# A decoder layer on one core: x kept on chip, queries stored in three parts, denominators spread by a product, a middle stage three chunks deep, weights transposed by the host

## The chip, the core and the metric

The kernel runs on one core of one Trainium2 chip. A core has a matrix engine (TensorE, PE in the profile, its weight loads as PEld), a vector engine (DVE), an activation engine (ACT), a general engine (POOL) and a sync engine (SP) that issues most DMA transfers here. Each engine runs its own instructions in the order written, and they meet through semaphores. The metric is the device time of one execution in microseconds (us), lower is better. Before the change it is 1234.29 us, the median of three runs (1232.31 to 1235.03).

## The reference

One pre-norm decoder layer over 4 sequences of 1024 tokens, 256 features, 16 heads of 16. Where the given mask is true, the score is set to -1e9.

```python
def self_attn(x):                       # x normalised
    Q, K, V = x @ Wq.T + bq, x @ Wk.T + bk, x @ Wv.T + bv        # (b, s, 16, 16)
    scores = (gt * einsum(Q, W_cross, K) + (1 - gt) * einsum(Q, M @ K)) * 16 ** -0.5
    # M: 16 x 16 a head, shift_weights at offsets 0 to 7; gt = sigmoid(gate)
    scores = where(causal, scores, -inf)
    return (softmax(scores) @ V) @ Wo.T + bo
def cross_attn(x, ctx, masked):         # ctx: 77 tokens a sequence
    q, k, v = x @ Wq, ctx @ Wk, ctx @ Wv
    return (softmax(where(masked, -1e9, q @ k.T / 4)) @ v) @ Wo
def ffn(x):                             # hidden 768, int32 weights / 127
    return (silu(x @ wg.T) * (x @ wu.T)) @ wd.T
x = x + self_attn(norm(x)); x = x + cross_attn(norm(x), ctx, mask); x = x + ffn(norm(x))
```

## The kernel before

The 4096 tokens are worked on as 8 chunks of 512, and attention as 16 groups of 4 heads (4 groups for each sequence). The program is a row of blocks. At the end of each all engines meet, so nothing of a block starts before every engine has left the one ahead; the function `barrier` adds such a meeting at the same places.

1. **Weights** (0 to about 50 us). All inputs are loaded. The projection weights are transposed on TensorE (L489) and emptied by ACT (L444) and DVE (L382). `W_cross`, the shift weights and the gate are folded into the query weights (DVE L387 to L415). Keys and values of the context are made. The FFN's integer weights are converted (ACT L450), transposed, and split in a high and a low part. ACT and PE begin when all loads up to the cross-attention weights have landed.
2. **Q/K/V chunks** (50 to 134.7 us). For each chunk x is loaded, normalised (DVE L215), transposed (L1208), and multiplied by the weights (L178). Queries and keys are split in three bf16 parts that add up to the f32 value; values get a column of ones (L1128 writes them, `a_vst`, 32 columns a head of which 17 hold data). All goes to DRAM (`qk`, `vs`).
3. **Self-attention** (134.7 to 668.2 us). For each group, a ring of 40 units of *maxima* (L753 for scores, L762 for the causal part, then the DVE maximum L677), whose row `self_mrow` travels by DMA (L627) into two extra rows of the queries `self_stq`. Then 38 *score* units (L776, L784), for which ACT takes the exponential (L728), and 12 sets of *value products* (L796): the exponentials stream against f32 value tiles `self_va` of 32 columns, four heads side by side. ACT empties a set (L720), SP stores it (L649, `od`, numerators and denominators). SP loads the groups' inputs with L958, L962 and L869: 19 transfers a group.
4. **Middle** (668.2 to 801.2 us). For each chunk the quotients `oin` x `din` are made (L909; `din` is the inverse denominators, which a DMA L845 has read from DRAM once for each of the 16 columns of a head). Then the projection (L986), the residual sum (L1415, with x loaded again as `rin`), moments (L157 to L168), a power on POOL (L1369), the normalisation (DVE L1429), transposes (L1500), transposes of the mask (L1506), and the query product (L1516), split in three bf16 parts (L1483, L1436, L1439, L1374). The parts are stored in six slots by 48 transfers from the queues of SP and ACT (L1299), and the new x is stored too (L1326). Two chunks are under way at a time. DVE also works out which tokens are fully masked (L1401 to L1406), with padding of a sequence to 96 context columns.
5. **Cross-attention** (801.2 to about 964 us). The same ring as in stage 3, without the causal part, on 96 context columns a head, L758 adding the mask.
6. **FFN** (to 1233.9 us). The denominators, the projection and the normalisation of `c`, then the three large products (L178) for each chunk.

What sets the order around the change: each engine's own list, written by hand as loops (`chunk c`, `unit u`), and the meetings between blocks. The class `ChunkInputs` (L873) holds the loads of `oin`, `din` and `rin`, the quotients and the projection for both stage 4 and stage 6; its `early_...` methods run a first chunk's part inside the attention block's last group. SP's list in the last group of stage 3 or 5 thus holds the loads of the next stage's first two chunks (L843, L845, L903), at the last two of four points:

```python
                if i == 2:
                    sp.wait_ge(self.s_inv, 32)
                    self.load(sp, 0, 0)
                if i == 3:
                    self.load(sp, 0, 1)
```

## Time and profile before

| | before |
|---|---|
| median of three runs | 1234.29 us |
| profiled execution | 1235.59 us |
| span of its trace | 1233.9 us |
| mean granted TensorE clock | 0.947 of full speed |
| PE busy, PEld busy | 1076.2 us (87%), 633.6 us (51%) |
| DVE, ACT, POOL busy | 788.9, 556.0, 215.9 us |

The span runs from the first to the last instruction in the trace, and the profiled execution's own time is 1.7 us longer. In the rows below, *windows* give the busy time of each engine in a stretch with its number of instructions, then the granted TensorE clock as a share of full speed, the busy share of the DMA engines, and GB/s. A *timeline* row is: start, duration, engine, line, operation, out<-in, count (neighbouring instructions of one kind are one row), and in brackets the idle time ahead with what ended it. A row of *lines by form* is one kind of instruction in a stretch: busy us in all and mean ns of one, then the engine's idle us ahead of it and what released it. *Waits* give us in all, times and the longest. A matrix product in f32 appears as two passes, so x16 in a timeline is 8 products in the program.

### The profile page before, as it was taken

How to read it: one execution, taken by the hardware profiler on the slowest of the kernel's cores; microseconds unless marked ns; L12 is line 12 of the kernel's file. 1: busy time of each engine (PE TensorE's matmuls, PEld its weight loads, DVE VectorE, ACT ScalarE, POOL GpSimd, SP SyncE). 2: the span in 40 equal slices, each digit the busy share in tenths (PEclk: the TensorE clock that was granted, in tenths of full speed). 3: DMA queues.
4: the chain of work that ended last, by engine and by line, in shares of the span. 5: the costliest groups of instructions: out<-in, count | busy, mean ns of one | idle time of the engine just before them, and what ended most of it. 6: DMA issues, size and time to landing. Idle time of an engine off the chain costs nothing. (4 is left out here: it accounts for less than half of the span.)

```text
span 1233.9 us, 19626 instructions
## 1 busy us (share of the span) xinstructions
PE 1076.2 (87%) x7164; PEld 633.6 (51%) x7164; DVE 788.9 (64%) x1705; ACT 556.0 (45%) x1022; POOL 215.9 (17%) x175
## 2 busy tenths in 40 slices
PE   1889969999999999999997656669999599999997
PEld 1677424444444444444433434334444278888886
DVE  4699847777777777777872757655556254554452
ACT  2455126666666666666674111216666321111110
POOL 4155510000000000000001334310000133333321
PEclk9899769999999999999999887779999789999999
DMA  6389993434443344443022786865664422222200
GB/s 198 98 286 306 271 150 75 82 86 84 87 89 86 86 86 85 82 88 80 23 75 86 207 240 187 244 217 179 177 182 131 158 61 69 69 70 69 69 18 35
DMA packets 132831, 153.28 MB, mean 124 GB/s; under 512 B 29003, under 2 KB 104319, under 8 KB 132735
## 3 DMA queue, kind: packets, MB, share of 16 engines
q1 hardware_dynamic: 126207, 145.74, 45.5%
q10 hardware_dynamic: 6528, 6.29, 1.5%
q8 instruction: 57, 0.93, 0.3%
q14 instruction: 39, 0.32, 0.1%
HBM read 87.69 MB, written 64.95 MB: 124 GB/s over the span
## 5 line engine op out<-in xcount | busy, mean ns | idle before, releaser
L677 DVE TENSOR_REDUCE self_pm<-bank 128x1 f32<-128x512 f32 (+3 forms) x608 | 365.0, 657 | 95.4 <-PE bank L762 74.5
L728 ACT ACTIVATE self_prob<-bank 128x512 f32<-128x512 f32 (+1 forms) x608 | 325.6, 577 | 170.7 <-PE bank L784 97.0
L776 PE MATMUL bank<-self_stq,self_stk 98*128 98x512 bf16 (+3 forms) x768 | 223.1, 331 | 16.0 <-DMA self_stq<-self_mrow 10.7
L753 PE MATMUL bank<-self_stk,self_stq 96*128 96x512 bf16 (+3 forms) x768 | 227.4, 339 | 9.1 <-DVE self_mrow L674 6.6
L796 PE MATMUL bank<-self_prob,self_va 128*32 128x512 f32 (+3 forms) x1536 | 161.4, 500 | 0.0
L753 PEld LDWEIGHTS bank<-self_stk,self_stq 96*128 96x128 bf16 x768 | 70.6, 99 | 160.9 <-DVE self_pm L677 114.2
L951 POOL TENSOR_TENSOR rin<-rin,bo_b 128x1024 f32<-128x1024 f32 x8 | 26.1, 3260 | 528.0 <-DMA min_<-mask_BxSxS_bk 528.0
L1758 ACT ACTIVATE e_sg<-bank 128x512 f32<-128x512 f32 x48 | 28.8, 599 | 192.1 <-PE bank L178 192.1
L776 PEld LDWEIGHTS bank<-self_stq,self_stk 98*128 98x128 bf16 x768 | 69.6, 99 | 75.4 <-issue 20.7
L728 ACT ACTIVATE cross_prob<-bank 96x512 f32<-96x512 f32 x128 | 74.5, 591 | 60.6 <-PE bank L781 60.4
L677 DVE TENSOR_REDUCE cross_pm<-bank 128x4 f32<-128x384 f32 x128 | 69.5, 557 | 33.3 <-PE bank L758 31.8
L762 PE MATMUL bank<-tri_q,identb 128*128 128x128 bf16 (+2 forms) x352 | 88.1, 250 | 0.0
L784 PE MATMUL bank<-tri_k,identb 128*128 128x128 bf16 (+2 forms) x352 | 86.4, 245 | 0.0
L986 PE MATMUL bank<-wo_t,oin 128*128 128x256 f32 x128 | 42.2, 501 | 45.9 <-DVE oin L909 40.6
L178 PE MATMUL bank<-e_xnt,wg_t 128*128 128x512 f32 x288 | 78.5, 408 | 1.4 <-DVE e_xnt L1711 1.4
L1674 POOL TENSOR_TENSOR e_ht<-e_hf,e_ht 128x512 fp32r<-128x512 f32 x48 | 62.6, 1303 | 76.7 <-DVE e_ht L1705 76.7
L178 PE MATMUL bank<-e_xnt,wu_t 128*128 128x512 f32 x288 | 75.8, 398 | 0.0
L178 PE MATMUL bank<-wd_t,e_ht 128*128 128x256 f32 x576 | 70.5, 282 | 3.2 <-POOL e_ht L1674 3.2
L178 PEld LDWEIGHTS bank<-wd_t,e_ht 128*128 128x128 f32 x576 | 70.1, 188 | 4.3 <-POOL e_ht L1674 3.7
L1703 DVE TENSOR_TENSOR e_hf<-bank,e_sg 128x512 f32<-128x512 f32 x48 | 33.1, 690 | 54.2 <-ACT e_sg L1758 42.3
L986 PEld LDWEIGHTS bank<-wo_t,oin 128*128 128x128 f32 x128 | 32.6, 262 | 57.6 <-DVE oin L909 45.6
L178 PEld LDWEIGHTS bank<-e_xnt,wu_t 128*128 128x128 f32 x288 | 54.8, 190 | 13.5
(189 smaller groups left out, 1418.0 us busy)
## 6 DMA issues: line engine op xcount, KB each, us to landing
qk<-a_parts SPq DMA_DIRECT2D x32, 384.0 KB, 4.9
self_stq<-qk SPq DMA_DIRECT2D x192, 64.0 KB, 3.0
self_stk<-qk SPq DMA_DIRECT2D x96, 128.0 KB, 5.2
cross_stq<-xqs SPq DMA_DIRECT2D x32, 384.0 KB, 4.7
vs<-a_vst SPq DMA_DIRECT2D x8, 1024.0 KB, 7.2
self_va<-vs SPq DMA_DIRECT2D x16, 512.0 KB, 7.3
od<-self_u SPq DMA_DIRECT2D x16, 512.0 KB, 2.6
oin<-od SPq DMA_DIRECT2D x32, 256.0 KB
```

Of the source, the lines that this page charges most:

```text
L178: mm = nc.tensor.matmul(dst, a[:, i], b[:, j], start=(n == 0), stop=(n == 3 * len(terms) - 1))
L677: nc.vector.tensor_reduce(pm[:, k, h0:h0 + hb, r], src[:, 0:hb * w].rearrange("p (h w) -> p h w", h=hb), AX, ALU.max).then_inc(s_mxe, 1)
L728: nc.scalar.activation(ops.prob[:, u % NPS, 0:hb * n], bank[ST_BANKS[u % 3]][0:KP, 0:hb * n], ACT.Exp).then_inc(s_ex, 1)
L753: mm = nc.tensor.matmul(dst[:, h * w:(h + 1) * w], stq[i][0:R, half, h0 + h, r * P:(r + 1) * P], stk[i][0:R, h0 + h, k0:k0 + w], start=(h ...
L762: mm = nc.tensor.matmul(dst[:, 0:hb * w].rearrange("p (h w) -> p h w", h=hb)[:, :, w - P:w], identb[:], tri_q[:, 0:hb], start=False, stop= ...
L776: mm = nc.tensor.matmul(dst[0:KP, h * n:(h + 1) * n], stk[i][0:RM, h0 + h, kt * KP:(kt + 1) * KP], stq[i][0:RM, half, h0 + h, q0:q0 + n], ...
L784: mm = nc.tensor.matmul(dst[:, 0:hb * n].rearrange("p (h n) -> p h n", h=hb)[:, :, 0:P], identb[:], tri_k[:, 0:hb], start=False, stop=True ...
L796: mm = nc.tensor.matmul(bank[PV_BANKS[half]][h * VW:(h + 1) * VW, q0:512], va[i][:, kt, h * VW:(h + 1) * VW], ops.prob[:, (first + h // hb ...
L986: mm = nc.tensor.matmul(bank[w][:, i * D:(i + 1) * D], oin[:, u, k, (2 * w + i) * P:(2 * w + i + 1) * P], wo_t[:, k], start=(k == 0), stop ...
L1674: nc.gpsimd.tensor_tensor(ht[:, u, 1, h], hf[:, h % 2], ht[:, u, 0, h].bitcast(F32), ALU.subtract).then_inc(s_hl, 1)
L1703: nc.vector.tensor_tensor(hf[:, h % 2], bank[5 + 2 * (h % 2)][:], sg[:, h % 2], ALU.mult).then_inc(s_h, 1)
L1758: nc.scalar.activation(sg[:, h % 2], bank[4 + 2 * (h % 2)][:], ACT.Silu).then_inc(s_sg, 1)
```

## The change

- **Weights.** The host hands over `Wk`, `Wv`, `Wo`, the FFN weights, the context and the mask already transposed, so the transposes of block 1 go. SP and ACT both issue the loads, in another order, and the gate is among the first. The conversion of the FFN weights moves into the middle stage (ACT makes the high part, POOL the low part).
- **x kept on chip.** x is loaded once into `xres` (8 chunks), POOL adds the bias, the residual sums are made in place. The loads `rin` and the stores `x1s` go.
- **Values.** `a_vst` and `va` hold 17 columns a head instead of 32, with the four heads innermost: the columns of one head's weight tile lie 16 bytes apart in memory instead of side by side.
- **Self-attention.** A group's inputs come by 10 transfers instead of 19. Groups 0 and 1 are loaded during the q/k/v chunks, 2 and 3 from ACT's queue. The banks of the ring carry on over a group's end, and the last value products of a group are issued among the first units of the next.
- **Denominators.** A bf16 product of the inverses `rd` with a 0/1 matrix `sel` (L922) writes the spread inverses into a bank, and DVE multiplies from there (`quotients`).
- **Middle.** The projection runs three chunks ahead of the query product. Normalisation is on ACT, POOL makes power and offset, the mask comes as one tile, the queries go out in three parts by 2 transfers a chunk. In the last self-attention group six spreads and two projections run ahead (before: one projection).
- **Cross-attention** works on 80 context columns, keys and mask of all groups are resident, and the FFN's first inputs are loaded after group 6 of the 16.

```diff
@@ layout and DRAM tensors
-    SK = 96
+    SK = 80
+    VC = HD + 1
-    x1s = dram("x1s", (NCH, P, J, D), F32)
-    xqs = dram("xqs", (B, KT, len(Q_PARTS), HD, HP, S), BF16)
+    rd3 = dram("rd3", (B, 3, H, S), BF16)
+    xq3 = dram("xq3", (B, KT, 3, P, S), BF16)
+        xres = sb(root, "xres", [P, NCH, J, D])
@@ weights: the transposes on TensorE go, the host does them
-            turned(n_k, both(wk_t), KT, KT)
-            turned(n_v, both(wv_t), KT, KT)
-            turned(n_o, (wo_t,), KT, KT)
-            turned(fg, both(wg_t), KT, HT)
-            turned(fu, both(wu_t), KT, HT)
-            turned(fd, both(wd_t), HT, KT)
+        ("Wk_t", rows_first(given["L0_attn_Wk"].T)),
+        ("Wv_t", given["L0_attn_Wv"].T),
+        ("Wo_t", given["L0_attn_Wo"].T),
+        ("gate_t", given["L0_ffn_w_gate"].T),
+        ("up_t", given["L0_ffn_w_up"].T),
+        ("down_t", given["L0_ffn_w_down"].T),
@@ values: 17 columns a head, heads innermost
-            vst = sb("a_vst", [P, 2, GB, J, HG, VW])
+        vst = sb(qkv, "a_vst", [P, 2, GB, J, VC, HG])
@@ loads of a self-attention group
-            for slot, part in enumerate(Q_PARTS):
-                for c in range(2):
-                    sp.dma_start(stq[HD * slot:HD * (slot + 1), c],
-                                 qk3[0, part, bass.ds(g, 1), :, c * 512:(c + 1) * 512]
-                                 .rearrange("a (h r) t -> (a r) h t", h=HG)).then_inc(ld, 16)
+            for slot, first, number in Q_RUNS:
+                for c in range(2):
+                    eng.dma_start(stq[i][HD * slot:HD * (slot + number), c],
+                                  qk3[0, b, i // 2, first:first + number, :, c * 512:(c + 1) * 512]
+                                  .rearrange("c (r h) s -> (c r) h s", h=HP)[:, heads]).then_inc(ld[i], 16)
@@ SP at the start of self-attention
-                barrier(sp, 2)
-                load_group(sp, self_ops, 0, 1)
-                self_sync(sp, True)
-                load_group(sp, self_ops, 0, 2)
-                self_sync(sp, False)
+                qkv_sync(sp)
+                barrier(sp, 1)
+                self_sync(sp)
+            for i in range(2, GB):
+                a.wait_ge(s_set, i + 1)
+                load_self(a, i)
@@ order of the products, and the bank of a unit
+            plan += [("p", s, -1) for s, x in enumerate(sets) if x[3] - 1 == NST + u - LAG]
-                    dst = bank[MX_BANKS[n % 3]]
+                dst = bank[MXB[N % NMB]]
+        early(8, lambda t: spread(t, 0, 0))
+        early(10, lambda t: spread(t, 0, 1))
+        early(13, lambda t: project2(t, 0))
+        early(15, lambda t: spread(t, 1, 0))
+        early(18, lambda t: spread(t, 1, 1))
+        early(22, lambda t: project2(t, 1))
+        early(26, lambda t: spread(t, 2, 0))
+        early(30, lambda t: spread(t, 2, 1))
@@ denominators by a product
-                eng.tensor_tensor(oin[:, u], oin[:, u], din[:, u], ALU.mult).then_inc(self.s_on, 1)
+        def spread(t, c, k):
+            b, u = c // 2, c % 2
+            t.wait_ge(s_rl, 16 * (b + 1))
+            n = KT * c + k
+            need(t, s_on, n if c < N_EARLY else n - 1)
+            nc.tensor.matmul(bank[EB if c < N_EARLY else BB[k]][:], sel[:, k], rd[:, b, u * CH:(u + 1) * CH],
+                             start=True, stop=True).then_inc(s_bc, 1)
+        def quotients(v, c, k):
+            v.wait_ge(ldo[c % 3], 32 * (c // 3 + 1))
+            v.wait_ge(s_bc, KT * c + k + 1)
+            nc.vector.tensor_tensor(oin[:, c % 3, k], bank[EB if c < N_EARLY else BB[k]][:], oin[:, c % 3, k],
+                                    ALU.mult).then_inc(s_on, 1)
@@ middle stage
-                for slot, number in Q_RUNS:
-                    eng.dma_start(xqs[bass.ds(b, 1), n, slot:slot + number, :, :, u * CH:(u + 1) * CH]
-                                  .rearrange("a s r h t -> (a r h) s t"),
-                                  parts[:, u, n, 0:number]).then_inc(so[n][u], 16)
+                sp.dma_start(xq3[b, n, :, :, u * CH:(u + 1) * CH].rearrange("c p s -> p c s"),
+                             cparts[:, u, n]).then_inc(cso[u], 16)
+            t.wait_ge(s_u, 2 * G)
+            t.wait_ge(s_on, KT * N_EARLY)
+            for k in range(KT):
+                spread(t, 3, k)
+            project2(t, 2)
+            turn(0)
+            for c in range(NCH):
+                t.wait_ge(cs_xt, KT * (c + 1))
+                for n in range(KT):
+                    need(t, cs_r, KT * (c - 1) + n + 1)
+                    for k in range(KT):
+                        mm = nc.tensor.matmul(bank[QB[n]][:], xwq[:, k, n * P:(n + 1) * P], cxnt[:, c % 2, k],
+                                              start=(k == 0), stop=(k == KT - 1))
+                    mm.then_inc(cs_q, 1)
+                if c + 4 < NCH:
+                    for k in range(KT):
+                        spread(t, c + 4, k)
+                if c + 1 < NCH:
+                    turn(c + 1)
+                if c + 3 < NCH:
+                    project2(t, c + 3)
+            t.wait_ge(cs_xt, KT * NCH)
+            t.wait_ge(cs_r, KT * NCH)
+                    for k in range(KT):
+                        quotients(v, c + 4, k)
+                if c + 3 < NCH:
+                    sums2(v, c + 3)
+        def mid_scalar(a):
+            def normalise(c):
+                a.wait_ge(cs_nm, c + 1)
+                need(a, cs_tr, KT * (c - 1))
+                for j in range(J):
+                    nc.scalar.activation(cxn[:, c % 2, j], xres[:, c, j], ACT.Identity,
+                                         scale=crstd[:, c % 3, j:j + 1],
+                                         bias=cneg[:, c % 3, j:j + 1]).then_inc(cs_xn, 1)
@@ inputs of the last stage
-                if i == 2:
-                    sp.wait_ge(self.s_inv, 32)
-                    self.load(sp, 0, 0)
-                if i == 3:
-                    self.load(sp, 0, 1)
+                    store_inverse(sp, b)
+                    if b == 0:
+                        load_ffn(sp, 0)
+                        load_ffn(sp, 1)
```

TensorE's list in the middle stage, two chunks of the kernel before (`oin` are the quotients, `c_xn` the normalised chunk, `c_xnt` its transpose, `c_meff` the mask):

```order
L986 MATMUL bank<-wo_t,oin 128x256 x8
L1500 MATMUL bank<-ident,c_xn 128x128 x8
L1506 MATMUL bank<-identb,c_meff 96x128 x4
L1516 MATMUL bank<-c_xnt,xwq 128x512 x4
L986 MATMUL bank<-wo_t,oin 128x256 x8
L1500 MATMUL bank<-ident,c_xn 128x128 x8
L1506 MATMUL bank<-identb,c_meff 96x128 x4
L1516 MATMUL bank<-c_xnt,xwq 128x512 x4
```

The same engine and stage after the change, from its first row on (`rd` are the inverse denominators, `sel` the 0/1 matrix):

```order
L922 MATMUL bank<-rd,sel 128x512 x2
L937 MATMUL bank<-wo,oin 128x256 x8
L1097 MATMUL bank<-ident,c_xn 128x128 x8
L1112 MATMUL bank<-c_xnt,xwq 128x512 x4
L922 MATMUL bank<-rd,sel 128x512 x2
L1097 MATMUL bank<-ident,c_xn 128x128 x8
L937 MATMUL bank<-wo,oin 128x256 x8
L1112 MATMUL bank<-c_xnt,xwq 128x512 x4
```

Before, a chunk's projection, transposes and query product follow one another. After, the row L937 is for the chunk three ahead of the query product L1112 behind it, and the transposes are for the next one.

SP's list where self-attention begins, before (from the last store of the q/k/v chunks to the loads of group 1):

```order
L1079 DMA vs<-a_vst 128x4x512
L958 DMA self_stq<-qk 16x4x512 x12
L962 DMA self_stk<-qk 16x4x1024 x6
L869 DMA self_va<-vs 128x1024
L627 DMA self_stq<-self_mrow 1x16x128 x2
L958 DMA self_stq<-qk 16x4x512 x12
L962 DMA self_stk<-qk 16x4x1024 x6
L869 DMA self_va<-vs 128x1024
L627 DMA self_stq<-self_mrow 1x16x128 x2
```

and after:

```order
L248 DMA qk<-a_parts 128x3x512 x4
L251 DMA vs<-a_vst 128x4x272
L676 DMA stq<-mrow 1x16x128 x8
L681 DMA od<-u_out 128x1024
L663 DMA stq<-qk 48x4x512 x2
L663 DMA stq<-qk 32x4x512 x2
L663 DMA stq<-qk 16x4x512 x2
L667 DMA stk<-qk 48x4096
```

The maxima's transfers (L627, now L676) no longer have 19 loads of a group ahead of them on SP: the first loads stand earlier in the list, inside the q/k/v stores, and two groups' loads are on ACT's list.

TensorE's list in the last self-attention group, after (`prob` are the exponentials, `va` the values, `tri_k` the causal part):

```order
L814 MATMUL bank<-stq,stk 128x384
L818 MATMUL bank<-tri_k,identb 128x128
L922 MATMUL bank<-rd,sel 128x512
L814 MATMUL bank<-stq,stk 128x256 x2
L818 MATMUL bank<-tri_k,identb 128x2x128
L814 MATMUL bank<-stq,stk 128x256 x2
L818 MATMUL bank<-tri_k,identb 128x2x128
L922 MATMUL bank<-rd,sel 128x512
L814 MATMUL bank<-stq,stk 128x128 x4
```

The spreads L922 stand between score units, as do two projections further on.

## Rows read from the trace of the kernel before

**Rows 1.** Windows: us; busy us of PE, PEld, DVE, ACT, POOL; clock; DMA; GB/s.
```profile
134.70:165.00 30.30, 20.64 (x71) 5.66 (x72) 22.93 (x45) 0.00 (x0) 13.96 (x5) 0.59 0.91 241
165.00:668.20 503.20, 488.47 (x3753) 209.25 (x3753) 365.54 (x680) 338.70 (x639) 5.76 (x2) 0.98 0.40 82
668.20:818.90 150.70, 88.19 (x355) 57.04 (x356) 98.89 (x261) 22.55 (x41) 48.48 (x34) 0.82 0.73 221
818.90:964.00 145.10, 134.72 (x1079) 66.59 (x1079) 77.55 (x199) 86.95 (x154) 0.00 (x0) 0.97 0.58 163
964.00:986.50 22.50, 9.57 (x39) 5.65 (x39) 6.97 (x17) 3.50 (x7) 5.66 (x3) 0.71 0.45 155
986.50:1233.90 247.40, 238.51 (x1328) 207.51 (x1328) 118.64 (x249) 38.14 (x65) 83.79 (x61) 0.98 0.20 57
```

**Rows 2.** Timeline, DVE and PE at the start: start, us, engine, line, names.
```profile
14.25 0.24 DVE L387 TENSOR_SCALAR ge<-ge 128x2 f32<-128x2 f32 x1 [14.25 <-ACT ge L440]
...
22.75 0.29 DVE L415 TENSOR_TENSOR ablk<-ablk,blk 128x128 f32<-128x128 f32 x1
...
46.95 1.06 PE L1208 MATMUL bank<-ident,a_xn 128*128 128x128 f32 x8 [3.05 <-SPq L1031]
50.22 5.28 PE L178 MATMUL bank<-a_xnt,wq_t 128*128 128x512 f32 x12 [2.20 <-DVE a_xnt L1101]
```

**Rows 3.** Timeline of DVE and PE in a chunk of the q/k/v stage.
```profile
62.23 1.41 DVE L1128 TENSOR_TENSOR a_vst<-bank,bv_b 128x256 f32<-128x256 f32 x4
...
65.86 1.09 PE L1208 MATMUL bank<-ident,a_xn 128*128 128x128 f32 x8 [1.02 <-DVE a_xn L215]
```

**Rows 4.** Timeline of SP's queue ahead of self-attention.
```profile
158.03 5.73 SPq L958 DMA_DIRECT2D self_stq<-qk  x12
```

**Rows 5.** Waits of PE, 134 to 668: total us, times, longest.
```profile
PE bank L776 <- DMA self_stq<-self_mrow: 10.7, 2, 7.9
PE bank L753 <- DVE self_mrow L674: 6.6, 15, 1.0
PE bank L776 <- ACT self_prob L728: 4.9, 18, 0.3
```

**Rows 6.** Lines by form, 300 to 580: busy us, mean ns | idle us.
```profile
L796 PE MATMUL bank<-self_prob,self_va 128*32 128x512 f32 x432 | 57.5, 605 | 0.0
...
L796 PEld LDWEIGHTS bank<-self_prob,self_va 128*32 128x32 f32 x864 | 17.9, 108 | 31.3 <-ACT self_prob L728 16.8 <-issue 12.9
```

**Rows 7.** Timeline of PE in the middle stage.
```profile
705.37 3.72 PE L986 MATMUL bank<-wo_t,oin 128*128 128x256 f32 x16 [1.82 <-DVE oin L909]
709.90 1.09 PE L1500 MATMUL bank<-ident,c_xn 128*128 128x128 f32 x8 [0.81 <-DVE c_xn L1429]
...
711.79 3.70 PE L1516 MATMUL bank<-c_xnt,xwq 128*128 128x512 f32 x8 [0.57 <-ACT c_xnt L1473]
...
742.79 6.29 PE L986 MATMUL bank<-wo_t,oin 128*128 128x256 f32 x16 [8.37 <-DVE oin L909]
```

**Rows 8.** Lines by form, 667 to 802 us.
```profile
L986 PE MATMUL bank<-wo_t,oin 128*128 128x256 f32 x112 | 38.5, 518 | 45.9 <-DVE oin L909 40.6 <-DVE c_x L1415 5.3
...
L157 DVE BATCH_NORM_STATS2 c_stat<-c_x 128x6 f32<-128x256 f32 x32 | 11.2, 414 | 0.3
...
L1415 DVE TENSOR_TENSOR c_x<-bank,rin 128x512 f32<-128x512 f32 x16 | 10.2, 678 | 0.3 <-issue 0.3
...
L1473 ACT ACTIVATE c_xnt<-bank 128x512 f32<-128x512 f32 x16 | 8.7, 594 | 86.9 <-PE bank L1500 86.9
...
L1369 POOL TENSOR_TENSOR c_rstd<-c_ve,mhalf 128x4 f32<-128x4 f32 x8 | 8.1, 1017 | 35.6 <-DVE c_ve L168 35.6
```

**Rows 9.** Lines by form, 819 to 964 us.
```profile
L753 PE MATMUL bank<-cross_stk,cross_stq 96*128 96x96 bf16 x448 | 37.7, 207 | 7.3 <-DVE cross_mrow L674 5.1 <-DMA cross_mk<-mts 2.2
L758 PE MATMUL bank<-negid,cross_mk 96*128 96x384 bf16 x112 | 37.1, 331 | 0.0
```

**Rows 10.** Timeline of POOL behind cross-attention.
```profile
969.52 2.34 POOL L909 TENSOR_TENSOR oin<-oin,din 128x1024 f32<-128x1024 f32 x1 [163.66 <-DMA rin<-x1s]
```

More of the change, by code:

```diff
@@ L529, in attention @@
-        def attention(stage, name, causal, ahead, ops, o_dst, following):
-            KW = S if causal else SK
-            KP = P if causal else SK
-            NKT = S // P if causal else 1
-            NPS = 12
-            mx_units = []
+        s_xh = sem("a_xh")
+        s_xt = sem("a_xt")
+        s_qk = sem("a_qk")
+        s_hi = sem("a_hi")
+        s_r = sem("a_r")
+        s_m = sem("a_m")
+        s_lo = sem("a_lo")
+        s_vm = sem("a_vm")
+        s_ve = sem("a_ve_")
+        so = sems("a_so", 2)
@@ L559, in attention @@
                     st_units += [(half, kt, h, hb, q0, n, diag) for h in range(0, HG, hb)]
-                    sets.append((half, kt, first, len(st_units), kt == kts[0], kt == kts[-1], q0, n, hb))
-            NST = len(st_units)
-            half_end = [max(s[3] for s in sets if s[0] == h) for h in range(2)]
-            ring = [("m", i) for i in range(len(mx_units))]
-            ring.insert(min(n_half + (4 if causal else 2), len(ring)), ("t", 0))
-            ring.append(("t", 1))
-            NMX = len(ring)
@@ new lines, in cross_scalar, with outputs @@
+        def cross_scalar(a):
+            def outputs(g, c):
+                if c == 0:
+                    need(a, xus[g % 2], 16 * (g // 2))
+                a.wait_ge(xs_pv, g * NST2 + HG * (c + 1))
+                nc.scalar.activation(xu[:, g % 2, c * 512:(c + 1) * 512], bank[PVB[c]][:],
+                                     ACT.Identity).then_inc(xs_u, 1)
+            for g in range(G):
+                for u in range(NST2):
+                    U = g * NST2 + u
+                    a.wait_ge(xs_st, U + 1)
+                    need(a, xs_pv, U + 1 - NPS2)
+                    nc.scalar.activation(xprob[:, U % NPS2], bank[STB[U % NSB]][0:SK, :], ACT.Exp).then_inc(xs_ex, 1)
+                    if u == NST2 - 1:
+                        outputs(g, 0)
+                    if g and u == LAG2:
+                        outputs(g - 1, 1)
+            outputs(G - 1, 1)
@@ L1361, in _ @@
+        cross_left.close()
+        cross.close()
+        last = root.enter_context(ExitStack())
+        yo = sb(last, "e_yo", [P, 2, J, D])
+        exnt = sb(last, "e_xnt", [P, 2, 2, KT, CH], F32R)
+        sg = sb(last, "e_sg", [P, 2, CH])
+        hf = sb(last, "e_hf", [P, 2, CH])
+        ht = sb(last, "e_ht", [P, 2, 2, HT, CH], F32R)
+        with nc.Block() as block:
+            @block.sync
+            def _(sp):
+                ffn_sync(sp)
                 barrier(sp, 4)
```

2768 lines of the change are left out of this document (1373 added, 1395 removed).

## The prediction

> **What bounds the kernel now.** I read the span in windows first [rows 1]. In self-attention, cross-attention and the FFN PE is busy nearly all the time: 488.5 of 503.2 us, 134.7 of 145.1 and 238.5 of 247.4, at a clock of 0.97 or 0.98. An edit there pays only if it takes work off PE. The rest is where PE waits: the head, up to 50.22 us, when the first q product runs [rows 2]; the entry to self-attention, 134.7 to 165, 20.6 busy of 30.3 at a clock of 0.59; the middle stage with the meeting behind it, 668.2 to 818.9, 88.2 busy of 150.7; and the passage to the FFN, 9.6 of 22.5. Second, the waits of PE and the rows by line say what ends the idle time, and third the timelines give one pass of each loop. In all of them the reader is to see the idle time in brackets and the name behind it: in the middle stage nearly all of it is the quotients `oin` (45.9 us, 40.6 of them L909) [rows 8], which are late because their inputs come through DRAM.
>
> **The head.** DVE starts folding at 14.25, held by ACT's gate row L440, and ends the fold at 22.75 + 0.29, 8.8 us for some 20 dependent rows [rows 2]. ACT waited for all loads up to the cross-attention weights. Afterwards the gate is the third kind of load and nothing else is waited for; I take 7 for DVE's start, half of 14.25, since half of the loads stand ahead of it. The two folds are interleaved, so I take 8.3 instead of 8.8: done at 15.5. What stood between the fold and the first transposes at 46.95 was nearly all weight transposes and the integer weights, which go. What stays are the statistics, the power on POOL, the normalisation and the context products. Statistics are four of 0.41 us [rows 8] and six small rows of about 0.2 (an estimate from the 0.24 of L387), the power 1.0 [rows 8], normalisation about as long as the statistics: 1.7 + 1.2 + 1.0 + 1.7 = 5.6, so transposes at 21. From the transposes to the first q product it took 50.22 - 46.95 = 3.3 [rows 2]; with context products of about 2 between, the first q product stands at 26. That is 24 us earlier. Bounds: 18 (start at 10, the context products in the way with their copies) and 28.
>
> **The q/k/v chunks.** x is there already, the products are the same. One idle gap of 1.02 us a chunk [rows 3] could go (8 x 1.02 = 8 gained); against that the writes of the values, 1.41 us a chunk [rows 3], are now at a pitch of four elements and could take twice as long, 8 x 1.4 = 11 lost if nothing covers them. I take 0, nearest to the products that do not change, and keep +11 and -8.
>
> **Entry to self-attention.** PE waited twice, 10.7 us in all, for rows of the maxima that travel by SP [rows 5]; SP had 12 transfers of L958 in front, 5.73 us [rows 4], and six of L962 behind. After the change SP has only the maxima's transfers at its head. I count -10.7; up to 8 more could come if PE's 20.6 busy us in rows 1 at a clock of 0.59 run at 0.98 (20.6 x (1 - 0.59/0.98)), and up to 2 could be lost on ACT, whose 20 transfers stand ahead of exponentials.
>
> **Group boundaries.** PE waited 15 times for `self_mrow`, 6.6 us, and 18 times for ACT's exponentials, 4.9 us [rows 5]: one each at the 15 borders between groups, and the others beside them. The ring carries on over the border now. Of the 11.5 I count 9.
>
> **Value products.** The weight tile has 17 columns instead of 32, 16 bytes apart. A load took 108 ns, its product 605 [rows 6], and the load is covered by the product ahead in most sets. I take 0: fewer columns, each of them costlier. Half of the 864 loads' 17.9 us in rows 6 is 9, for a window of 280 of 503 us, so 16 over the stage is the largest gain if none were covered; I take 13 to either side. The Trainium skill speaks against this edit: "Advanced Engine Details and Errata", section Memory Cachelines, has lines of 16 bytes in SBUF, of which two hits each are needed for full speed and where a new line for each access costs extra. By that rule every column of a load is on a line of its own, where before four shared one; by the row alone (108 ns, covered) nothing is lost. No trace of before has a strided load, so none can say how much. What such a penalty would need to turn the result is the slower rival below.
>
> **Last self-attention group.** One more projection (3.72 for a chunk, rows 7) and six spreads come in, 3.7 + 6 x 0.2 = 5. A spread is one bf16 product of 512 columns; from L753 with 96 columns, 207 ns, to L758 with 384, 331 ns [rows 9], a column costs 0.43 ns, so 0.22 us. Count +5; both ends 3 and 7.
>
> **The middle stage.** For a chunk PE has the projection 3.72, the transposes 1.09, the query product 3.70 [rows 7] and two spreads 0.44; the mask's transposes go. That is 8.9 us, if the projection runs three ahead and nothing is late. DVE has two quotients and two sums (each like L1415, 0.68), statistics 4 x 0.41, six small rows of 0.2, two splits of 0.68: 6.8 us, so DVE is close behind but covered. POOL's power and multiplication take 2 x 1.02 [rows 8] against 1.02 before, ACT's two copies of the transposes (L1473) 2 x 0.59. Walk: meeting 1.3 us, spreads and a projection 4.1, transposes 1.1 and copies: the first query product ends at about 11. The loads of the outputs of chunk 3 are issued only when the last group's stores have landed, 8 us in, and DVE takes the quotients of chunk 3 ahead of the sums of chunk 2, so the second is later than PE's pace: about 19. Four chunks at 8.9 follow: 19 + 4 x 8.9 = 54.6. The last two have no projections but their own copies and sums, 7.9 and 6.6, and a last product with its split and stores 3.7: 73. The two stages before have 150.7 with the meeting [rows 1]; of these the entry to cross-attention I take at 16, for stores and maxima's transfers still stand there: 73 + 16 = 89, so -61.7. Bounds: 83 (PE's 8 x 8.9 = 71, less the projection of the head, + 14) and 125 (below). The cover is thin: the queries' split and DVE's order have two chunks of slack at most, and if it is gone, a chunk costs what the chain from quotients to normalisation costs.
>
> **Cross-attention.** 80 columns instead of 96 a head: 16 x 4 fewer in the score rows (L753) and as many in L758, 128 columns a unit, x 0.43 ns [rows 9] = 55 ns; 128 units: 7.0. The wait for `cross_mrow`, 5.1 [rows 9], goes with the continued ring. Count -12; bounds -4 and -14.
>
> **Passage to the FFN.** PE is busy 9.6 of 22.5 us [rows 1]. POOL began the quotients at 969.52, when `rin` had landed, after 2.34 us of work each chunk [rows 10]. With x resident and the first inputs loaded since group 6, the quotients can be made in the attention stage's last groups. What stays is the meeting, the chain of projection, sums, power, normalisation, transposes: 3.7 + 1.4 + 2.9 + 2 + 1.7 = 11.5. Count -11; bounds -4 and -13. The FFN itself (247.4) has the same products: 0.
>
> **Sum.** -24 + 0 - 10.7 - 9 + 0 + 5 - 61.7 - 12 - 11 = -123.4. The profiled execution took 1235.59, so 1112.2; the median of the runs stands 1.3 lower (1234.29), so 1110.9, say 1111. The measurement of this kernel can tell a change from none above about 0.2%, 2.5 us.
>
> **The rivals.** *A, the forecast:* 1095 to 1128, as worked out. *B, the middle stage does not reach PE's pace.* DVE at 6.8 us of 8.9 takes its work strictly in order, the spread for chunk c+4 waits for a bank that DVE empties, and ACT and POOL get the FFN weights' conversion on top (1536 columns three times each). If a chunk takes about 12 us, 8 x 3.1 = 25 are lost; if the loads of outputs come behind the queries' stores too, up to 36 more: 1128 to 1165. For it: in rows 7 the projection waits 8.37 us for DVE behind a long chain, and then runs slower (6.29 for the same 16 rows that took 3.72) at a stage clock of 0.82. Against it: three chunks of slack, and half the stores. *C, better:* the gaps of rows 3 go (8), loads of values shrink (13), the entry's clock rises (8): 1070 to 1095. *D, slower than before:* strided value loads on PE's path. There are 16 x 12 = 192 sets of 8 loads (four heads, two passes). To lose all 123 us, a set must take 0.64 us longer, or 80 ns a load if nothing covers it: a load of about 190 ns instead of 108 [rows 6]. From there on the kernel is slower; at 250 ns it takes 1111 + 192 x 8 x 0.142 = 1329. Against it: a load with covered start and 17 columns instead of 32 would need to cost more than three times as much a column. *E, part of the change does nothing:* the head stays (the FFN weights or x hold it) or the middle is bound by transfers throughout, 1165 to 1231.
>
> **How the numbers follow.** A 0.52, B 0.25, C 0.15, E 0.03, D 0.04, and 0.01 for a time within 0.2% of before. The prediction is A's, 1111. Range: all of A, most of B and of C, 1080 to 1152, leaving out a third of B, the last quarter of C, D and E, together 0.08 + 0.04 + 0.07, just under 0.2. Faster: A + B + C + E = 0.95, of which I move 0.01 to slower for other unseen faults: 0.94, within 0.2% 0.01, slower 0.05.
>
> **What would show it.** In the profile after: the first q product at 24 to 30 us; PE without a wait for a maxima row over 2 us at the entry; in self-attention the value loads' mean near 100 ns (D: near 200 or more) and the stage's busy share above 97%; in the middle stage one query product each 9 us from the second on, no wait of PE above 2 us, a clock above 0.82 (B: 12 us a chunk, PE idle by quotients or sums); the passage to the FFN at 11 to 12 us. I am wrong if the head's gain is under 15 or the middle's under 40, and in direction only by way of the value loads.

## The result and the profile after

The kernel after takes 1252.86 us (median of three runs, 1251.66 to 1254.38) against 1234.29 before. The ratio is 1.0155 with a 95% interval of 1.0129 to 1.018: slower by 1.6%, where 1111 was forecast and 1080 to 1152 was the range. The span of the profiled execution is 1251.1 us, and the mean granted clock is 0.87 instead of 0.947.

The windows of the kernel after, cut where the same work begins and ends as in [rows 1] (length, then busy us of PE, PEld, DVE, ACT, POOL, then clock, DMA share, GB/s):

```profile
33.35:116.60 83.25, 75.37 (x442) 64.09 (x440) 72.78 (x173) 47.32 (x78) 42.69 (x38) 1.00 0.76 223
116.60:642.80 526.20, 511.99 (x3846) 217.82 (x3846) 410.14 (x772) 341.25 (x641) 30.45 (x17) 0.97 0.37 76
642.80:749.20 106.40, 74.74 (x317) 45.00 (x317) 48.88 (x136) 54.14 (x88) 43.59 (x33) 0.84 0.57 156
749.20:1002.80 253.60, 241.51 (x1117) 100.84 (x1117) 76.99 (x214) 90.35 (x159) 5.70 (x3) 0.51 0.36 80
1002.80:1007.60 4.80, 1.12 (x12) 0.86 (x8) 2.64 (x6) 2.54 (x4) 0.00 (x0) 0.83 0.28 112
1007.60:1251.10 243.50, 236.06 (x1320) 208.69 (x1320) 116.74 (x246) 36.02 (x63) 83.61 (x61) 0.98 0.14 44
```

| stage | before | after | change | forecast |
|---|---|---|---|---|
| head, to the first q product | 50.2 | 33.35 | -16.9 | -24 |
| q/k/v chunks | 84.5 | 83.25 | -1.2 | 0 |
| self-attention | 533.5 | 526.2 | -7.3 | -14.7 |
| middle and entry to cross-attention | 150.7 | 106.4 | -44.3 | -61.7 |
| cross-attention | 145.1 | 253.6 | **+108.5** | -12 |
| passage to the FFN | 22.5 | 4.8 | -17.7 | -11 |
| FFN | 247.4 | 243.5 | -3.9 | 0 |

Every stage but one is shorter. Cross-attention alone takes 108.5 us more, at a granted clock of 0.51 of full speed where it was 0.97 [rows 1], although PE is busy 241.5 of 253.6 us. The same products by form, in cross-attention after:

```profile
L1339 PE MATMUL bank<-xstq,xstk 98*80 98x512 bf16 x119 | 75.7, 636 | 0.0
L1341 PE MATMUL bank<-mk,negid 80*80 80x512 bf16 x118 | 74.8, 634 | 0.0
```

The same two in cross-attention before:

```profile
L776 PE MATMUL bank<-cross_stq,cross_stk 98*96 98x512 bf16 x125 | 49.8, 398 | 4.3 <-PEq L1255 4.3
L781 PE MATMUL bank<-cross_mk,negid 96*96 96x512 bf16 x125 | 48.3, 386 | 0.0
```

They took 398 and 386 ns and now take 636 and 634, with 80 columns of weights instead of 96. The clock fell at the end of the middle stage and stayed at 1.2 GHz (0.50 of full speed) until the first projection of the FFN:

```profile
730.00:735.00 5.00, 3.72 (x41) 2.26 (x41) 3.98 (x12) 0.20 (x1) 1.67 (x2) 0.79 0.46 159
735.00:740.00 5.00, 4.44 (x39) 3.14 (x40) 3.75 (x12) 0.00 (x0) 0.00 (x0) 0.50 0.01 3
740.00:745.00 5.00, 0.66 (x6) 0.27 (x4) 1.34 (x4) 0.00 (x0) 0.00 (x0) 0.50 0.42 81
745.00:750.00 5.00, 0.79 (x2) 0.21 (x2) 0.00 (x0) 0.00 (x0) 0.00 (x0) 0.50 0.56 82
750.00:995.00 245.00, 233.69 (x1080) 96.92 (x1080) 73.38 (x200) 88.04 (x155) 4.69 (x2) 0.50 0.37 80
```

The projection's products have 128 rows and 128 columns of weights, and from 996 on the clock is 1.00 again:

```profile
994.21 4.38 PE L1454 MATMUL bank<-xwo,oin 128*128 128x256 f32 x16
```

The idle stretch from 740 to 749 is a wait for the maxima, and four waits for queries stand behind it, the longest of 6.7 us. Waits of PE in the kernel after, from 725 to 1000 us (total, times, longest):

```profile
PE bank L1339 <- DMA xstq<-xmrow: 8.6, 1, 8.6
PE bank L1326 <- DMA xstq<-xq: 7.9, 4, 6.7
```

The kernel before falls to the low clock at the same place, at about 816 us, and leaves it again after about 10 us. Its windows:

```profile
820.00:825.00 5.00, 2.84 (x15) 1.71 (x16) 1.06 (x3) 1.19 (x2) 0.00 (x0) 0.50 0.55 144
825.00:830.00 5.00, 5.00 (x39) 2.62 (x37) 2.77 (x7) 2.96 (x5) 0.00 (x0) 0.85 0.51 124
830.00:835.00 5.00, 4.45 (x41) 2.16 (x37) 2.36 (x7) 2.44 (x5) 0.00 (x0) 1.00 0.17 66
```

So the question was not why the clock fell, but why it did not come back. The change did two things to this stage that could matter: 80 columns and rows a head instead of 96, and another order of loads and waits.

### The profile page after: what moved, and what is told of

The parts are those of the page before. It is cut to its first block and busy times, and to the rows that moved or that the text cites. A ratio compares the mean times of both kernels' runs of the same rounds, so it can differ in the third digit from the quotient of the medians.

```text
span 1251.1 us, 19036 instructions
## 1 busy us (share of the span) xinstructions
PE 1151.4 (92%) x7092; PEld 645.8 (52%) x7092; DVE 748.7 (60%) x1603; ACT 577.7 (46%) x1043; POOL 230.2 (18%) x191
## 5 line engine op out<-in xcount | busy, mean ns | idle before, releaser
L726 DVE TENSOR_REDUCE pm<-bank 128x1 f32<-128x512 f32 (+3 forms) x608 | 364.6, 656 | 83.6 <-PE bank L802 63.4
L774 ACT ACTIVATE prob<-bank 128x512 f32<-128x512 f32 (+1 forms) x608 | 329.2, 575 | 184.0 <-PE bank L818 105.2
L797 PE MATMUL bank<-stk,stq 96*128 96x512 bf16 (+3 forms) x768 | 227.2, 340 | 7.3 <-DVE pm L726 4.1
L814 PE MATMUL bank<-stq,stk 98*128 98x512 bf16 (+3 forms) x768 | 222.4, 328 | 0.9 <-ACT prob L774 0.8
L828 PE MATMUL bank<-prob,va 128*17 128x512 f32 (+3 forms) x1536 | 164.0, 500 | 0.0
L1305 ACT ACTIVATE xprob<-bank 80x512 f32<-80x512 f32 x128 | 75.7, 592 | 181.6 <-PE bank L1341 181.3
L1339 PE MATMUL bank<-xstq,xstk 98*80 98x512 bf16 x128 | 80.7, 631 | 8.6 <-DMA xstq<-xmrow 8.6
L1341 PE MATMUL bank<-mk,negid 80*80 80x512 bf16 x128 | 80.4, 628 | 0.0
L132 PE MATMUL bank<-e_xnt,wg 128*128 128x512 f32 x288 | 76.7, 402 | 1.6 <-DVE e_xnt L1507 1.6
L132 PE MATMUL bank<-e_xnt,wu 128*128 128x512 f32 x288 | 74.4, 394 | 0.0
```

What stands on the lines that cost most here:

```text
L132: mm = nc.tensor.matmul(dst, a[:, i], b[:, j], start=(n == 0), stop=(n == 3 * len(terms) - 1))
L726: nc.vector.tensor_reduce(pm[:, k, h0:h0 + hb, r], src[:, 0:hb * w].rearrange("p (h w) -> p h w", h=hb), AX, ALU.max).then_inc(s_mxe, 1)
L774: nc.scalar.activation(prob[:, U % NPS, 0:hb * n], bank[STB[U % NSB]][:, 0:hb * n], ACT.Exp).then_inc(s_ex, 1)
L797: mm = nc.tensor.matmul(dst[:, h * w:(h + 1) * w], stq[i][0:R, half, h0 + h, r * P:(r + 1) * P], stk[i][0:R, h0 + h, k0:k0 + w], start=(h ...
L814: mm = nc.tensor.matmul(dst[:, h * n:(h + 1) * n], stk[i][0:RM, h0 + h, kt * P:(kt + 1) * P], stq[i][0:RM, half, h0 + h, q0:q0 + n], start ...
L828: mm = nc.tensor.matmul(bank[PVB[half]][h * VW:h * VW + VC, q0:512], va[g % GB][:, kt, :, h], prob[:, (g * NST + first + h // hb) % NPS, ( ...
```

## The experiments

A ratio is the time against the kernel before, measured beside it, with its 95% interval behind it. The diffs are cut to the lines that matter.

### First round: 80 or 96, and the idle stretch

Theory T1: products on 80 rows or columns don't bring the clock back once it has fallen. Rival T2: the clock stays down because of the idle stretch and the thin work ahead of the stage, whatever the tile. `a_sk96` is the kernel after with 96, `a_sk88` with 88, and `b_sk80` is the kernel before with 80; each is one line:

```diff
-    SK = 80
+    SK = 96
```

`a_fill8` puts products on the full array into the idle stretch at the entry:

```diff
+            for n in range(8):
+                nc.tensor.matmul(bank[PVB[1]][:], ident[:], xwo[:].rearrange("p k d -> p (k d)"), start=True, stop=True)
             for g in range(G):
                 for what, which, ahead in plan2:
```

> The kernel before with 80 context columns and rows a head in cross-attention instead of 96: that part of the change alone. T1: the clock, which falls to 0.5 around 820 us in the kernel before, doesn't come back in cross-attention, and the kernel takes 1330 to 1350 us. T2: it comes back as in the kernel before, and the kernel takes 7 us less, about 1227.

Measured: 1324.7 us (ratio 1.074, 1.070 to 1.078), a little under T1's range and 91 us slower than the kernel before beside it (1233.3). Its windows in cross-attention, the last of which takes in the first projection of the FFN:

```profile
810.00:820.00 10.00, 4.78 (x33) 2.45 (x30) 4.21 (x13) 0.59 (x1) 0.00 (x0) 0.50 0.87 248
820.00:840.00 20.00, 18.50 (x91) 8.33 (x92) 6.05 (x16) 6.53 (x11) 0.00 (x0) 0.50 0.31 85
840.00:1080.00 240.00, 228.04 (x1044) 97.49 (x1042) 76.61 (x203) 90.16 (x151) 5.66 (x3) 0.52 0.36 102
```

This is T1: with one constant changed and the old order of loads and waits, the clock stays at 0.5 for the whole stage (0.50 from 805 to 1060). The constant sets the rows and the columns of several products at once; no run tells which of them counts.

> The kernel after with 96 context columns and rows a head in cross-attention instead of 80, all else as it is. Theory T1 (products on 80 rows or columns don't bring TensorE's clock back once it has fallen): the stage runs at a clock near 1 again, about 145 us instead of 252, and the kernel takes 1135 to 1150 us. Theory T2 (the clock stays down because of the idle 8.6 us and the thin work ahead of the stage, whatever the tile size): clock 0.5 as before, and some 7 us more, about 1260.

Measured: 1252.33 us (ratio 1.0166, 1.0118 to 1.0215), no gain, with executions from 1247.8 to 1259.3. Both theories failed as written: the clock was neither near 1 nor at 0.5. It rose and fell again and again. Waits and windows of this run:

```profile
PE bank L1326 <- DMA xstq<-xq: 20.5, 9, 4.5
```

```profile
760.00:770.00 10.00, 9.14 (x79) 4.53 (x82) 5.71 (x15) 5.81 (x11) 0.00 (x0) 1.00 0.08 28
770.00:780.00 10.00, 5.86 (x42) 2.84 (x38) 2.92 (x8) 2.64 (x6) 0.00 (x0) 0.72 0.59 108
780.00:800.00 20.00, 19.69 (x90) 8.15 (x91) 6.15 (x15) 6.30 (x11) 0.00 (x0) 0.50 0.33 67
800.00:820.00 20.00, 19.69 (x96) 9.16 (x94) 7.29 (x19) 7.94 (x14) 0.00 (x0) 0.53 0.39 90
```

In the fast stretch PE has 9.1 us of work in 10, and then the queries of the group after next come late: PE waits 3.3 us for `xstq<-xq`, up to 776.8, and the clock falls. While the clock is low most of these loads are in time (no such wait from 777 to 818, and in the kernel after four waits of 7.9 us in all against nine of 20.5 here), so it hides the fault. So there is a second cause, which 80 columns had covered. The last two windows show a thing more: at 96 too PE was busy 39.4 of 40 us at the low clock, and it took until 818 to come back. What 96 has over 80 is that the clock did come back, after every fall but the last, 31 us ahead of the projection; it did not do so at once.

Part of the lateness comes from another piece of the change. With the queries stored in three parts instead of six slots, SP issues six transfers for a group where it issued two. The load in this run, then in the kernel before:

```profile
768.96 3.29 SPq L1210 DMA_DIRECT2D xstq<-xq  x6
```

```profile
853.79 1.11 SPq L969 DMA_DIRECT2D cross_stq<-xqs  x2
```

That is 2.2 us more; what of the wait of 3.3 us it makes was not tested apart from the place of the load in SP's list.

> The kernel after with eight f32 products of 128 x 128 x 512 put in front of the first scores of cross-attention, into a bank that nothing uses yet, where PE idles 8.6 us. T1: the clock rises during them and is back at 0.5 soon after, with 80 columns: 1250 to 1262 us. T2: with the idle stretch filled the clock stays up, about 1140 to 1150 us.

Measured: 1247.1 us (1.0108, 1.0075 to 1.0141), 3 us under T1's range. The clock rose and was 1.00 from 760 to 770 with 80 columns, then fell at the same wait for queries (3.9 us; 0.73 from 770 to 780, PE busy 5.4 of 10 us) and stayed at 0.50 to the end of the stage. T2 is out, and 80 columns did run at the high clock until a gap came.

> The kernel after with 88 context columns and rows a head. T1: either as with 96 (about 1140) or as with 80 (about 1256); a value between, by a stage partly at the low clock, is possible at the edge. T2: about 1256.

Measured: 1257.27 us (two executions), clock 0.50 in every window from 740 to 1000. 88 behaves as 80 does.

### Second round: a fifth query buffer

`n5_sk96` and `n5_sk80` load a group's queries one group earlier (the fifth buffer itself and the indices are left out here):

```diff
-        xld = sems("d_ld", GB)
+        NX = 5
+        xld = sems("d_ld", NX)
-                        load_cross(sp, g + GB - 1)
+                        load_cross(sp, g + NX - 1)
```

> The kernel after with 96 context columns and five query buffers in cross-attention instead of four, so that a group's queries are loaded one group earlier. Theory T1b (two causes: the late query loads let the clock fall again and again, and products on 80 rows never bring it back): no wait for xstq<-xq over 1 us, the clock near 1 for the whole stage, some 145 us for it instead of 252, the kernel 1135 to 1155 us. Rival T3 (the clock falls by the mix of the work itself, two groups ahead, whatever the waits): still 0.5 to 0.75 in many stretches, 1230 to 1250 us.

Measured: 1185.72 us (0.9593, 0.9552 to 0.9633), 67 us less than `a_sk96`, but 30 more than the top of T1b's range; the executions spread from 1178.6 to 1200.6. No wait for `xstq<-xq` was left. The clock was 1.00 from 760 to 810 and fell at two gaps, of 2.9 and 6.8 us; it was back after about 4 us in the first case and 24 in the second:

```profile
816.57 0.95 DVE L1408 RECIPROCAL den<-den 128x128 f32<-128x128 f32 x1 [4.85 <-DMA den<-od]
817.44 0.15 DVE L1266 COPY xmrow<-bank 32x128 bf16<-32x128 bf16 x1
...
817.64 0.34 PE L1328 MATMUL bank<-xstk,xstq 96*128 96x96 bf16 x4 [2.92 <-DVE xmrow L1266]
...
846.56 0.66 PE L1341 MATMUL bank<-xstq,xstk 98*96 98x512 bf16 x1 [6.80 <-DMA xstq<-xmrow]
```

First, DVE's reciprocal of the denominators waits 4.85 us for its load, and the copy that the maxima need is queued behind it. Second, both of the FFN's first chunks are loaded in one go, and SP's transfers of the maxima are queued behind them.

> The kernel after with five query buffers alone, 80 columns kept. T1b: the clock falls at the entry of cross-attention, as before, and doesn't come back although nothing is waited for: 1240 to 1252 us, the gain only the waits of 8 us. Rival T2b (without the late loads the clock comes back at 80 columns too): 1130 to 1150 us.

Measured: 1246.93 us (1.0115, 1.0083 to 1.0146): T1b. No wait for queries was left, and the clock stayed at 0.50 from 750 to 985.

> Five query buffers, 80 columns, and eight f32 products of 128 x 128 x 512 in the idle stretch at the entry. T1b in its form with memory (80 columns can't lift the clock but can hold it, as 760 to 770 us of the run with the filler alone suggest): the clock rises at the entry and stays at 1 through the stage, 1130 to 1145 us. The form without memory (80 columns can't hold it either; it falls some 10 to 20 us in): 1240 to 1250 us.

Measured: 1210.19 us (0.9809, 0.9784 to 0.9834): between the two forms, and its windows say why.

```profile
750.00:760.00 10.00, 10.00 (x56) 5.15 (x55) 2.93 (x8) 3.18 (x6) 0.00 (x0) 0.96 0.59 102
760.00:810.00 50.00, 45.37 (x403) 21.99 (x401) 26.34 (x76) 29.68 (x55) 0.00 (x0) 1.00 0.61 128
810.00:820.00 10.00, 6.37 (x40) 3.06 (x38) 3.64 (x9) 2.86 (x5) 0.00 (x0) 0.79 0.35 68
820.00:950.00 130.00, 128.05 (x586) 51.86 (x584) 39.26 (x107) 48.90 (x86) 4.70 (x2) 0.50 0.38 91
```

With 80 columns the clock stayed at 1.00 for 50 us with PE busy 45.4, fell at the gap of DVE's reciprocal, and did not come back in 130 us with PE busy 128. This is the form with memory: what counts in these runs is the clock at which the stage is entered and each gap behind it.

> As n5_sk96, and the conversion of the FFN weights stands three to four chunks later in the middle stage (chunks 5 to 7 instead of 1 to 3), and at the entry of cross-attention the transfers of the maxima stand ahead of the loads of group 3. If ACT's wait of 7.6 us for the weights' load and its conversions set the middle stage's pace (6.7 us wait of the query product at 689): 5 to 12 us less than n5_sk96 in the middle and 3 to 5 us at the entry. If the pace is set by the chain of a chunk (quotients to normalisation): under 4 us in all.

The edit in the middle stage (the same for POOL's half, and `c == 6` instead of `c == 2` for the last load), and at the entry `load_cross(sp, 3)` stands behind `maxima(1, 0)`:

```diff
-                if 1 <= c < 4:
-                    ffn_weight_high(a, c - 1)
+                if c >= 5:
+                    ffn_weight_high(a, c - 5)
```

Measured: 1173.38 us (0.9525, 0.9489 to 0.9561), 12 less than `n5_sk96`. The first scores of cross-attention stand at 746.5 instead of 752.6. The wait for maxima ahead of them is 3.7 us instead of 8.7, as expected; the last query product stands only 3.4 us earlier, where 5 to 12 were expected if ACT's wait set the pace. Counted from the first spread of the stage, the last query product stands 78.6 us in here, 82.3 in `n5_sk96` and 80.0 in the kernel after. The executions of both kernels spread over 8 us and more, and only one of each was profiled, so more than this isn't to be read from them.

### Third round: no gap left

`best96` is `n5_sk96_late` with

```diff
-                if b >= 0 and g % GB == 1:
+                if b >= 0 and g % GB == 2:
                     inverse(v, b)
-                if b >= 0 and g % GB == 2:
+                if b >= 0 and g % GB == 3:
                     store_inverse(sp, b)
-                    if b == 0:
-                        load_ffn(sp, 0)
-                        load_ffn(sp, 1)
+                if g in (8, 10):
+                    load_ffn(sp, (g - 8) // 2)
```

> n5_sk96_late with the two interruptions of cross-attention taken away: DVE's reciprocal of a sequence's denominators stands one group later (its load has landed by then), and the FFN's first loads stand in groups 8 and 10 instead of both in group 6, off the maxima's transfers. If the low clock in cross-attention comes only from such gaps (theory T1b): no wait of PE over 2 us after the entry, clock 1 from there to the end of the stage, which takes about 140 us, and the kernel about 1150 us (1173 less 4 us of waits and some 18 us of low clock). If the clock falls by itself in this stage: 1168 to 1175.

Measured: 1152.42 us (0.9332, 0.9314 to 0.935; all four within 3 us), as T1b said. Behind the entry PE's longest wait is 0.9 us, and the clock is 1.00 from 754 to the end of the stage:

```profile
PE bank L1323 <- DVE xmt L1275: 12.0, 14, 0.9
PE bank L1340 <- DMA xstq<-xmrow: 3.7, 1, 3.7
```

```profile
740.00:750.00 10.00, 6.27 (x37) 3.36 (x36) 4.72 (x14) 0.59 (x1) 0.00 (x0) 0.50 0.02 2
750.00:760.00 10.00, 9.14 (x65) 5.05 (x64) 5.07 (x14) 5.22 (x9) 0.00 (x0) 0.80 0.96 159
760.00:900.00 140.00, 128.19 (x1040) 63.55 (x1037) 76.25 (x199) 81.92 (x149) 4.72 (x2) 1.00 0.62 139
```

> The same with 80 columns and the eight filler products at the entry. T1b with memory: once lifted, the clock is held at 80 columns through the whole stage, since no gap is left: about 133 us for it and 1145 to 1152 us in all, with 7.4 us of filler partly in an idle stretch. If some short gap is enough at 80 columns, the clock falls at it and stays at 0.5 to the stage's end: 1180 to 1240 us.

Measured: three executions at 1146.2 to 1147.7 us (ratio of these three 0.9289, 0.9268 to 0.9309), and three at 1175.5 to 1178.0 with a mean clock of 0.937 instead of 0.967 to 0.969. Over all six the median is 1161.6, above the 1152.4 of `best96`: the 80 columns with their filler win 5 us when they hold the clock and lose 23 to 26 when they don't. Whether the three lost it within this stage isn't shown, since only one of the former was profiled. It had:

```profile
740.00:750.00 10.00, 8.82 (x14) 3.85 (x15) 0.77 (x3) 0.00 (x0) 0.00 (x0) 0.65 0.44 76
750.00:890.00 140.00, 126.75 (x1083) 60.45 (x1082) 72.92 (x200) 83.17 (x153) 4.72 (x2) 1.00 0.68 141
```

> best80 without the eight filler products: 80 columns, every gap of cross-attention taken away, and the clock at the entry left at 0.5. If the state at the entry decides (theory with memory): the clock stays at 0.5 to the end of the stage although nothing else differs from best80, some 250 us for it, 1240 to 1250 us. If the gaps were what kept it down in n5_sk80: it comes back, 1140 to 1160 us.

Measured: 1240.04 us (1.0066, 1.0045 to 1.0087). Only the eight products at the entry differ, and they are worth 92 us against the three faster executions of `best80`, 63 against the slower ones:

```profile
750.00:760.00 10.00, 9.76 (x49) 4.36 (x47) 3.60 (x11) 3.92 (x7) 0.00 (x0) 0.50 0.66 98
760.00:980.00 220.00, 216.83 (x1004) 88.49 (x1003) 71.08 (x185) 80.81 (x142) 4.68 (x2) 0.50 0.38 86
```

The Trainium skill, "TensorE: Matmul & The Clock Gate", section "What's actually happening", says that TensorE's clock follows how busy the engine has been of late. This run shows that busy time alone does not bring it back: PE was busy 216.8 of 220 us and stayed at the low level.

This kernel also differs from `best96` in the one constant alone, 80 against 96: 1240.0 against 1152.4, 88 us, close to the 91 of the kernel before.

> The kernel before with 80 columns and the eight filler products in front of the first scores of cross-attention, where it had 1324.7 us without them. With memory: the clock is lifted at the entry and held at 80 columns where PE has no gap; PE of the kernel before waits at most 0.4 to 0.9 us in this stage, so it should hold throughout: 1225 to 1240 us. Without: 1325 to 1335.

The same eight products stand in the kernel before, with 80 columns, ahead of the first scores. Measured: 1237.11 us (1.0033, 1.0019 to 1.0047), 88 us less than `b_sk80`, within the forecast, but not faster than the kernel before with its 96 (the interval lies above 1):

```profile
820.00:830.00 10.00, 9.69 (x19) 3.80 (x17) 0.21 (x1) 0.43 (x1) 0.00 (x0) 0.76 0.19 38
830.00:840.00 10.00, 9.26 (x85) 4.80 (x86) 5.24 (x15) 5.86 (x11) 0.00 (x0) 1.00 0.50 125
840.00:960.00 120.00, 111.80 (x972) 54.84 (x973) 64.65 (x184) 76.72 (x136) 0.00 (x0) 1.00 0.62 170
```

> best96, and in the middle stage ACT copies the transposes ahead of the second part of the queries, and makes the mask in four pieces (chunks 3 to 6) instead of one at chunk 4. If ACT's order is what delays the query products (waits for c_xnt of 1 to 4 us a chunk): 4 to 8 us less than best96. If the chain through sums and normalisation is: under 2 us.

```diff
+                if c + 1 < NCH:
+                    turned(c + 1)
                 for n in range(KT):
                     middle(c, n)
-                if c + 1 < NCH:
-                    turned(c + 1)
-                if c == 4:
-                    masks(a)
+                if 3 <= c < 7:
+                    masks(a, c - 3)
```

Measured: 1151.31 us (0.9324, 0.9307 to 0.9341) against 1152.42: 1.1 us, so ACT's order is not what is late there.

> The kernel after with the 17 value columns of a head side by side again instead of 16 bytes apart, the four heads outermost. Rival D of the prediction (strided loads are dear) would have the self-attention stage shorter by tens of us. By the trace of the kernel after (a load of 117 ns against 108 before) I expect loads near 105 ns and the time within 3 us of the kernel after's 1252.

The tile in self-attention; `a_vst` and the transfers between them change in the same way:

```diff
-                va.append(sb(scope, f"va{i}", [P, NKT, VC, HG]))
+                va.append(sb(scope, f"va{i}", [P, NKT, HG, VC]))
```

Measured: 1251.38 us (1.0132, 1.0112 to 1.0151), the same as the kernel after (1252.86). A load of value weights in self-attention, in the kernel after and in this one:

```profile
L828 PEld LDWEIGHTS bank<-prob,va 128*17 128x17 f32 x1256 | 25.5, 117 | 46.8 <-ACT prob L774 28.1 <-issue 18.7
```

```profile
L828 PEld LDWEIGHTS bank<-prob,va 128*17 128x17 f32 x1264 | 20.9, 95 | 47.1 <-ACT prob L774 28.4 <-issue 18.7
```

## Why the prediction was wrong

- **The step that failed is the term for cross-attention**, "Count -12; bounds -4 and -14". It multiplied saved columns by 0.43 ns, the price at full clock, and took the clock of 0.97 in [rows 1] for a property of the stage. It hung on the 96 rows and columns: with them the clock came back after the fall at the entry, and with 80 it did not. The term measured +108.5. The runs divide it: 80 columns alone cost 91 us in the kernel before (`b_sk80`) and 88 in the kernel after without its gaps (`best80_nofill` against `best96`). The late query loads and two more gaps cost about as much at 96 (`a_sk96` 1252 against `best96` 1152, of which some 12 by the middle stage and the entry). The two causes hide each other, so that undoing one of them alone gained nothing or 6 us (`a_sk96`, `n5_sk80`). Why 80 does not bring the clock back stays open: the runs show that it doesn't, and not which rows or columns would.
- **The slower rival was the wrong one.** D put it on strided loads of value weights, and the prediction named them as the only way to a slower kernel. They cost 22 ns a load (117 against 95), far below the 190 from which D began, and `a_va` without the stride is no faster beyond noise (1251.4 against 1252.9). The rule that the prediction took from the Trainium skill, "Advanced Engine Details and Errata", section Memory Cachelines, agrees in sign with these two loads; the time shows nothing of it. None of the prediction's other signs of being wrong fired: the head's gain was over 15, the middle's over 40.
- **The head**: -16.9 instead of -24, just outside the bound of -18. DVE began at 10.0, not 7, for ACT's gate row waited for `bq`; the normalisation took 3.26 us, not 1.7; and the context products, with a wait of 2.1 us for DVE's `kr`, stood between the transposes at 23.4 and the first q product at 33.35.
- **Self-attention**: -7.3 instead of -14.7. The DMA waits of [rows 5] did go, but PE waited 2.7 us for the last `a_vst`, 5.1 us for DVE's `mt` and 3.4 for its `pm` at the entry, which took their place.
- **The middle**: -44.3 instead of -61.7, inside its bounds (of which the lower, 83, is 81.5 by its own terms, 71 - 3.7 + 14). A chunk did not take 8.9 us but about 10.3 (query products from 662.5 to 724.5, six steps), three of the eight query products ran at a fallen clock (5.1 to 6.5 us instead of 3.7), and the passage from the last one to the first scores took 21 us instead of 16. The longest single wait was for ACT, as rival B had it, by a load and not by the work: ACT stood 7.6 us for the FFN weights with everything else queued behind, and PE then waited 6.7 us:

```profile
681.15 1.48 ACT L1185 ACTIVATE iw<-iw 128x1536 f32<-128x1536 int32 x1 [7.63 <-DMA iw<-up_t]
```

```profile
689.13 5.08 PE L1112 MATMUL bank<-c_xnt,xwq 128*128 128x512 f32 x8 [6.74 <-ACT c_xnt L1066]
```

  It was not what set the pace. With the conversions moved, the stage was only 1.4 us shorter than in the kernel after and 3.7 shorter than in `n5_sk96`, and another order on ACT gave 1.1 us. By these two runs what is left is the chain of a chunk, from the quotients through the sums to the normalisation; no run changed it, so this is argued and not shown. At the entry to cross-attention the wait for maxima of 8.6 us stood behind six query transfers on SP; 5.0 of it were won by moving these.
- **The passage to the FFN**: -17.7 instead of -11, since the projection runs inside the last group of cross-attention.
- **Right**: the q/k/v chunks, the value loads, and the sign of each term but one. With the forecast's -12 in place of the measured +108.5, the rest stands at 1252.9 - 108.5 - 12 = 1132, inside the range; this is a sum and no run. The best runs are 1152 (`best96`) and 1146 to 1148 in half the executions of `best80`.

## What to carry to other kernels

Before a tile of TensorE is made smaller, look in the windows for the places where the clock is low and for what ran when it came back, since the smaller tile may not bring it back: fewer columns at half the clock cost 91 us here, where 7 were to be won. A short wait that brings the clock down costs far more than its own length, so look for late transfers with the stage at full clock; at the low clock most of them hide. If an undo alone gains nothing, a second cause may stand behind it. A filler that holds the clock in one profiled execution isn't safe for it: `best80` was fast in three executions of six, `best96` in all.

## What the runs showed of the hardware that was not expected

- At 80 rows and columns a head TensorE stayed at 1.2 GHz with PE busy 216.8 of 220 us (`best80_nofill`), and at 88 from 740 to 1000. In the kernel after it came back within 2 us of the first products of 128 x 128 x 256 behind the scores (0.50 up to 995, 1.00 from 996).
- At 96 it came back to 2.4 GHz in every trace within this stage, but not at a fixed distance: about 10 us after the fall in the kernel before, 4 and 24 us in `n5_sk96`, and in `a_sk96` only after 41 us of nearly unbroken work (777 to 818).
- At 80 it kept 2.4 GHz for 140 us once eight f32 products of 128 x 128 x 512 had stood at the entry: 1240 against 1146 to 1148 us (in three executions of six), and 1324.7 against 1237.1 in the kernel before.
- One wait of 3.6 to 3.9 us ended this for the rest of the stage at 80 columns (`n5_sk80_fill`, `a_fill8`). At 96 the clock also fell at waits of 1.2 to 2.0 us that stood just behind one of 0.9 (`a_sk96`), while waits of at most 0.9 us left it at 1.00 through the whole stage (`best96`).
- A weight load of 17 f32 columns took 95 ns side by side and 117 ns with 16 bytes between them; 32 side by side took 108 [rows 6].
